# Filter pass of a convolution kernel: the border of image n ahead of the attention adds of the first quarter of image n+1 on VectorE

## What is computed

```python
out_dk = jax.vmap(dyn)(f_att, ker)
out_lk = _conv(f_att, lk_filter, pad=LK // 2)
out = jnp.concatenate([out_lk + out_dk, f_idt], axis=1)
x = x + _L0_conv_ref(_gn(x), ...)
x = x + _L1_conv_ref(_gn(x), ...)
```

## Time and profile before

| | |
|---|---|
| median of 3 runs | 2868.17 us (2864.01 to 2870.11) |
| the profiled execution | 2870.12 us, span 2868.3 us |
| TensorE / VectorE / ScalarE / GpSimd busy | 2618.0 / 2124.2 / 1055.1 / 876.4 us |
| mean granted TensorE clock | 0.932 |
| attention and border steps of the filter pass | about 1672 to 2143 us of the span |

### The profile page before, as it was taken

The page is one execution under the profiler, slowest core; times in us unless marked ns, Lnnn a source line. Parts: engine busy times, 40 slices in busy tenths (PEclk is TensorE's granted clock), DMA queues, the critical chain, the costliest instruction groups (busy, mean ns, idle before and its releaser), DMA issues. The chain is left out here.

```text
span 2868.3 us, 38892 instructions
## 1 busy us (share of the span) xinstructions
PE 2618.0 (91%) x12262; PEld 2095.6 (73%) x12262; DVE 2124.2 (74%) x2832; ACT 1055.1 (37%) x1641; POOL 876.4 (31%) x799
## 2 busy tenths in 40 slices
PE   5999999969998799999999598988947999999998
PEld 4777777758887688888887476766735777777776
DVE  5444444554454788888887888898868899999998
ACT  1211111111100689889998322222103333333332
POOL 6544444312220544444443854454101000000000
PEclk9999999978886899999999798999968999999999
DMA  8222222210000877777776224434442333333332
GB/s 150 67 78 76 75 75 76 54 34 6 13 13 15 187 220 217 220 217 221 214 215 170 85 105 150 150 135 165 151 172 89 105 113 92 104 113 93 101 118 59
DMA packets 288702, 338.04 MB, mean 118 GB/s; under 512 B 24816, under 2 KB 243824, under 8 KB 274288
## 3 DMA queue, kind: packets, MB, share of 16 engines
q1 hardware_dynamic: 280736, 334.74, 39.7%
q10 hardware_dynamic: 7888, 2.29, 0.5%
HBM read 211.60 MB, written 122.62 MB: 117 GB/s over the span
## 5 line engine op out<-in xcount | busy, mean ns | idle before, releaser
L168 PE MATMUL ps_all<-vh,u_h 128*128 128x512 f32 x960 | 385.2, 401 | 29.5 <-DVE vl L2822 28.6
L170 PE MATMUL ps_all<-vh,u_l 128*128 128x512 f32 x960 | 383.1, 399 | 0.0
L169 PE MATMUL ps_all<-vl,u_h 128*128 128x512 f32 x960 | 382.5, 398 | 0.0
L2731 ACT ACTIVATE vh<-rt,gn 128x528 fp32r<-128x528 f32 x192 | 130.7, 730 | 446.8 <-DVE rt L2799 255.1
L168 PE MATMUL ps_all<-vh,t_h 128*128 128x512 f32 x576 | 231.2, 401 | 23.8 <-DVE vl L1874 23.8
L168 PEld LDWEIGHTS ps_all<-vh,u_h 128*128 128x128 f32 x960 | 180.7, 188 | 84.4 <-issue 38.0
L169 PE MATMUL ps_all<-vl,t_h 128*128 128x512 f32 x576 | 229.9, 399 | 0.0
L170 PE MATMUL ps_all<-vh,t_l 128*128 128x512 f32 x576 | 228.9, 397 | 0.0
L1713 POOL TENSOR_TENSOR zr<-zr,z 128x256 f32<-128x256 f32 x128 | 124.2, 990 | 342.3 <-DMA xr<-in_x 342.3
L170 PEld LDWEIGHTS ps_all<-vh,u_l 128*128 128x128 f32 x960 | 180.8, 188 | 46.2
L169 PEld LDWEIGHTS ps_all<-vl,u_h 128*128 128x128 f32 x960 | 181.0, 189 | 45.4
(11 more groups left out here) (407 smaller groups left out, 6851.2 us busy)
## 6 DMA issues: line engine op xcount, KB each, us to landing
xr<-in_x SPq DMA_DIRECT2D x128, 256.0 KB, 3.6
x_layer<-xr SPq DMA_DIRECT2D x64, 512.0 KB, 2.7
xq<-x_layer SPq DMA_DIRECT2D x32, 1024.0 KB, 4.9
x_layer<-xq SPq DMA_DIRECT2D x32, 1024.0 KB, 3.8
out<-ot SPq DMA_DIRECT2D x64, 512.0 KB, 5.3
xw<-in_x SPq DMA_DIRECT2D x112, 288.0 KB, 4.3
xc<-in_x SPq DMA_DIRECT2D x120, 256.0 KB, 3.9
xw<-x_layer SPq DMA_DIRECT2D x16, 1152.0 KB, 8.7
```

What stands on the lines that cost most here:

```text
L168: pe.matmul(o, wh, xh, start=first, stop=False, skip_group_check=True)
L169: pe.matmul(o, wh, xl, start=False, stop=False, skip_group_check=True)
L170: return pe.matmul(o, wl, xh, start=False, stop=last, skip_group_check=True)
L2731: act.activation(vh[:, v % 2, n, :, :].rearrange("p a b -> p (a b)"), rt[:, n, :, :].rearrange("p a b -> p (a b)"), ACT.Identity, scale=gn ...
```

## The change

`add_attention(a, 0)` is called behind `border(s)`, directly ahead of `add_attention(a, 1)`, on VectorE alone. No instruction is added or taken away. In the old order `border(s)` reads `rowr` and the first 16 entries of `colr` after `add_attention(a, 0)` has put the rows and columns of image a = s + 1 there; in the new order they still hold those of image s.

```diff
@@ VectorE, period(i, a, s, n)
                         if s is not None:
                             spread(s)
-                        if a is not None:
-                            add_attention(a, 0)
                         if i is not None:
                             outputs(i, 0)
...
                         if s is not None:
                             border(s)
                         if a is not None:
+                            add_attention(a, 0)
                             add_attention(a, 1)
                             low_lk(a, 3)
```

## The result

The changed kernel takes **2905.13 us** (median of 4 runs, 2902.46 to 2910.46), the kernel before 2868.89 (4 runs): ratio 1.0135 [1.0117, 1.0154], 36 us slower. The forecast was 2918, its range 2882 to 2938. The two profiled executions lie 40.4 us apart in span (that of the changed kernel is the slowest of its four), and I account for these 40.4.

What follows compares the result with a forecast made beforehand. TensorE's waits for VectorE between attention 1 and 2 were taken as the bound. Five full periods +35, without s +9.6, without n +4, the last +1.4: +50 us, against the median 2868.2 giving 2918, range 2882 to 2938.

Steps and rivals of the forecast that it cites:

- Waits removed: Between attention 1 and 2, TensorE's waits for outputs(i, 0) and rowf both go, 6.1 us per full period.
- Wait added: Attention 1 waits 16.2 us for quarter 0's adds, ending at T + 21.2; T is the end of component 2.
- Turns: VectorE's low_lk and sums alternate with GpSimd's operations, each waiting until the other's current one is over, lengthening VectorE's chain.
- Rival B: No turns between VectorE and GpSimd: chain ends T + 13.0 to T + 15.6, 2871 to 2884 us; chance 0.14.
- Clock: TensorE's matmuls after attention 1's wait run partly at the lower clock, losing 2.2 us per full period.
- Rival D: TensorE's clock stays low through border and component 5: 5.3 us lost instead of 2.2, 2934 us; chance 0.12.
- Full periods: The five full periods' stretches from attention 1 to 2 take 163.5 us against 128.3, +35.
- At no cost: Quarter 0's store and quarter 2's load go some 16 us later, yet quarter 2 arrives before its adds.
- Period without s: The period with no border in VectorE's chain: 13.0 us wait, 26.1 us against 16.5, +9.6.
- Without n: The period with neither sums nor GpSimd work: a wait of 2.4 us and clock loss of 1.6, +4.
- The last: The period without i and n: VectorE now also waits for lh and the square root, +1.4 us.
- Rival C: Faster: two waits merge into one at attention 1, chain T + 13.0, no clock loss, 2856 us; chance 0.04.

Runs made afterwards that it cites:

- the early border: Kernel before with the border, then quarter 0's two copies, moved directly behind the variance, ahead of low_lk and the sums; adds and statistics stay: 2844.77 us, ratio 0.9941.

## Why the prediction was right

The direction, the mechanism and the range were right; the size was 50 against 40.4 in the profiled executions and 36 in the medians. By its steps:

- **Waits removed**: right. Component 4 waits for nothing in the full periods, and the border follows it directly.
- **Wait added, 16.2 us with the adds ending at T + 21.2**: measured 15.33 to 15.47 and T + 20.4 (1763.35). `low_lk` ended at T + 3.1 (3.3 in the prediction), the first sum at T + 6.3 (6.7), the fourth at T + 10.7 (11.5), `low_dynamic` at T + 13.2 (14.0); the border took 3.2, as taken, and the adds 4.0. The 0.8 too much lies in GpSimd's side of the turns: its three operations after the first took 3.61, 2.49 and 1.40 us, 0.7, 0.3 and 0.2 more than in the earlier trace rows (the first full period, like the earlier trace rows), where I had counted a whole VectorE operation of 1.0, 0.5 and 0.45 us ahead of each; the last ended at T + 9.8 instead of 10.55.
- **Turns**: shown by the hold of GpSimd, 7.3 us a period, where the prediction made it T + 21.2 less T + 13.0 with the short border, 8.2. No row had shown `low_lk` or the first sum held up; both were. The rule of the Trainium skill by which VectorE's instructions with two inputs in SBUF and GpSimd's reads exclude each other (SBUF — State Buffer, Who interferes with whom) is borne out: the sum took 3.19 us beside GpSimd and 0.54 with it held. Rival B, which let them run free, falls.
- **Clock, 2.2 us a period**: measured 16.6 - 14.3 = 2.3. Rival D, a clock that stays low through border and component 5, falls: the border's 20 matmuls took 1.31 us, and the matmuls at the lower clock are those of attention 1 and the first of component 4.
- **Full periods, +35**: measured +31.6, by the 0.8 us of the wait.
- **At no cost**: right for the transfers. Behind attention 2 of the full periods TensorE takes 10.9 us to attention 3 and 15.8 to the next attention 0 in either kernel, without a wait.
- **Period without s, +9.6**: measured +9.3. **Without n, +4**: +2.4; the wait was 2.31 as predicted (2.4), but the clock loss of 1.6 was not there (granted clock 1.00); with GpSimd held the same wait at the same place did lose that much, so this part could as well have come out as forecast. **The last, +1.4**: +1.8.
- **Rival C**, faster, would have needed the chain at T + 12.7. Even the kernel with GpSimd held only reached T + 13.1 (1746.22, with T at 1733.16), where 1.0018 [1.0006, 1.0031] is no gain.

**The step that failed** is the sentence "Outside these stretches TensorE follows its own queue, and a us that a stretch gains or loses is a us of the span." I had read the waits by their two largest entries and placed all of TensorE's waits of the pass in the seven stretches. The list also had one of 3.6 us for `outputs(i, 2)`, and its period was 44.09 us long where the changed kernel needs 37.77. VectorE was late there, so what delays TensorE upstream of it is free up to that lateness: 6.3 us of the 9.3, shown by the kernel that changes this period alone. With it the sum would have been 44. Of the 9.6 us by which the forecast of 50 lies above the 40.4, 6.3 are this step and 3.6 the full periods; the other differences cancel.

Of the expectations behind the prediction, the early border gained half of what was expected, and two missed because they took a wait away and priced what came next at its old place: the copies behind the border (the next operations met GpSimd instead) and the hold of GpSimd with the early border (ScalarE's queue was stuck instead).

The 1.6 us by which the first stretch already starts later are not from the change. 0.6 of them are there when the first component of the filter pass starts (1601.67 before, 1602.29 after), and in the second profile of the changed kernel it starts at 1601.48. The other 1.0 arises behind a wait at 1632 us, in a period without an attention step, where both orders are the same: 12 matmuls ran at the lower clock there, 7 before; in the other profiles of orders that are alike up to there it is 6 to 13.

What stays open is what decides how many matmuls run at the lower clock after a wait: the five full periods of the changed kernel lost 1.6 to 2.9 us each after waits that were alike within 0.2 us.

## What to carry to other kernels

What a move brings is decided by what the moved work now stands behind: quarter 0's adds had slack at their old place, and in the new one a chain of thirteen VectorE instructions, with ScalarE and GpSimd in it, stood between component 2 and them. Where two engines take turns, look at which instructions collide and who waits behind them, not at busy shares. Under the copies the overlap cost component 4 a wait; with the copies moved away it fell on the next operations, and the border waited instead (1.0025). It became cheap only where what stood behind it had time left before TensorE needed it (0.9941). And list every wait of the stretch ahead of a predicted loss, small ones too, since a loss of one engine is paid back where another is late.

## What the runs showed of the hardware

- The loss of clock after a wait of attention 1 doesn't grow with the wait. In the five full periods attention 1 to attention 2 took 15.96 to 17.27 us (16.5 on average) after waits of 15.3 to 15.5 in the changed kernel, and 15.84 to 17.22 (16.5) after waits of 8.0 to 8.2 with GpSimd held; 14.33 is the need at the higher clock.
- Nor does the length of a short wait decide by itself. In the period without n attention 1 waits 2.31 us in the changed kernel and with GpSimd held alike. In the changed kernel the stretch behind it runs at a granted clock of 1.00 and takes 14.30 us:

```profile
2099.07 0.50 PE L2547 MATMUL ps_all<-lh,ga_h 32*128 32x512 f32 x4 [2.31 <-DVE xq L2378]
```

With GpSimd held it runs at 0.89 and takes 15.85 us, with single matmuls of 0.63 us:

```profile
2052.48 0.61 PE L2549 MATMUL ps_all<-lh,ga_h 32*128 32x512 f32 x4 [2.31 <-DVE xq L2380]
```

- The first matmul after a wait doesn't tell the clock of those behind it. With the early border and GpSimd held, the one after a wait of 3.56 us took 0.47 us, and the seventh, 1.6 us later, 0.63 (1783.12 and 1784.72).
- Even a copy of two elements per partition is held up: the one into `ms` took 0.95 us beside GpSimd and 0.17 with it held. The adds into `xq`, whose other input is in PSUM, are not: they took 4.00 us with GpSimd held until the first of them and so beside its 2.88 us difference, and 3.96 in the changed kernel, where GpSimd had stopped at 1758.63.
